# Gates by tanh, two layer norms applied on another engine, a second head copied by VectorE, and loops in another order

## What is computed

```python
x = x + attn(layernorm(x), Wq, Wk, Wv, Wo)           # the 16 heads of one token attend to each other
x = x + xattn(layernorm(x), ctx, Wq, bq, Wkv, bkv, Wp, bp)
#   q, k rounded per head to 127 steps, v per column, softmax over all 2048 keys,
#   probabilities rounded to 255 steps; 16 heads x 2048 queries x 2048 keys
x = x + moe(layernorm(x), gate, expert_bias, w1, w2, w3, shared_w1, shared_w2, shared_w3)
#   scores = sigmoid(x @ gate.T); the 2 of 8 experts with the largest score + bias
#   out = shared expert + sum over the chosen experts of w2(silu(w1 x) * (w3 x))
```

## Time and profile before

| what | value |
|---|---|
| time, median of 3 runs | 1123.94 us (1122.27 to 1124.36) |
| the profiled execution | 1121.76 us, of which its span is 1119.9 us |
| first scores kept (end of set-up) | 92.3 us |
| one tile in the steady part | about 63.1 us |
| VectorE, ScalarE, GpSimd, TensorE busy | 84%, 81%, 79%, 80% |
| mean granted TensorE clock | 0.98 |

### The profile page before, as it was taken

How to read it: one execution, slowest core, us unless ns; L and a number is a source line. 1 busy time by engine, 2 the same in 40 slices (tenths; PEclk the granted TensorE clock), 3 DMA queues, 4 the chain that set the end, 5 groups by cost and what they waited for, 6 DMA issues and landing times.

```text
span 1119.9 us, 30149 instructions
## 1 busy us (share of the span) xinstructions
PE 890.8 (80%) x11283; PEld 616.6 (55%) x11424; DVE 936.5 (84%) x1817; ACT 911.9 (81%) x1085; POOL 883.4 (79%) x890
## 2 busy tenths in 40 slices
PE   7956778787887878787887878787887878788786
PEld 4543446565555656565555556565655556556455
DVE  4967788888988888888988888898988888898883
ACT  2646889888888889888888889888888989889892
POOL 7669978897979888898979889898979888854040
PEclk9976999999999999999999999999999999999998
DMA  6011000000000000000000000000000000000000
GB/s 215 2 38 43 6 2 6 1 7 7 6 6 7 6 7 6 2 6 7 6 7 6 7 1 12 1 7 6 7 6 6 7 2 6 2 6 2 6 2 11
DMA packets 8438, 14.00 MB, mean 12 GB/s; under 512 B 1635, under 2 KB 6246, under 8 KB 7910
## 3 DMA queue, kind: packets, MB, share of 16 engines
q1 hardware_dynamic: 8294, 12.06, 3.2%
HBM read 9.96 MB, written 2.10 MB: 11 GB/s over the span
## 4 chain that ended last, share of the span: by engine, by line
PE 41%; issue 17%; ACT 15%; DVE 13%; POOL 12%; POOLq 1%; DMA 0%; DVEq 0%; SPq 0%; ACTq 0%
PE ps_score L1445 10%; PE ps_score L1456 9%; DVE score L1087 8%; PE ps L1310 7%; ACT prob L791 6%; ACT prob_t L803 5%; PE ps_pv L1472 4%; POOL routed_both L508 3%; PE ps L1519 2%; POOL gate L464 2%; PE ps_score L1310 2%; ACT queries L776 2%; POOL folded L545 1%; PE ps L1398 1%; PE ps L1549 1%
## 5 line engine op out<-in xcount | busy, mean ns | idle before, releaser
L1087 DVE TENSOR_SCALAR_CACHE_REDUCE score<-ps_score,q_neg 128x1024 f32<-128x1024 f32 x512 | 644.7, 1281 | 73.5 <-PE ps_score L1445 66.4
L791 ACT ACTIVATE prob<-score,exp_bias 128x2048 uint16<-128x2048 f32 x256 | 514.0, 2008 | 16.5 <-DVE exp_bias L1097 16.4
L1445 PE MATMUL ps_score<-keys,queries 128*128 128x512 bf16 x883 | 276.1, 382 | 114.9 <-ACT prob_t L803 73.2
L803 ACT COPY prob_t<-ps_score 128x1024 int32<-128x1024 int32 x240 | 242.8, 1012 | 80.5 <-PE ps_score L1456 77.8
L1456 PE MATMUL ps_score<-ident_f,prob 128*128 128x128 f16 x4096 | 272.1, 220 | 33.9 <-issue 30.0
L1456 PEld LDWEIGHTS ps_score<-ident_f,prob 128*128 128x128 f16 x4096 | 239.4, 98 | 96.5 <-issue 73.0
L545 POOL TENSOR_TENSOR folded<-product 128x512 f32<-128x512 f32 x128 | 161.7, 1271 | 42.9 <-DVE hs L1023 33.9
L1445 PEld LDWEIGHTS ps_score<-keys,queries 128*128 128x128 bf16 x1024 | 70.8, 97 | 201.1 <-issue 151.7
L535 POOL TENSOR_TENSOR product<-hs_exp,v_tok 128x1024 f32<-128x1024 f32 x64 | 149.0, 2350 | 14.0 <-ACT hs_exp L759 14.0
L535 POOL TENSOR_TENSOR product<-qk_rot 128x1024 f32<-128x1024 f32 x64 | 149.3, 2344 | 0.2 <-POOL qk_rot L528 0.2
L553 POOL TENSOR_TENSOR folded<-folded 128x256 f32<-128x256 f32 x128 | 92.2, 738 | 0.0
(11 more groups left out here) (144 smaller groups left out, 1225.6 us busy)
## 6 DMA issues: line engine op xcount, KB each, us to landing
prob_t<-in_w SPq DMA_DIRECT2D x3, 1024.0 KB, 4.8
x_in<-in_x SPq DMA_DIRECT2D x16, 128.0 KB, 2.0
score<-in_cond_t SPq DMA_DIRECT2D x4, 512.0 KB, 6.5
out<-x_out SPq DMA_DIRECT2D x16, 128.0 KB, 1.7
w_qkv<-in_w_qkv SPq DMA_DIRECT2D x1, 768.0 KB, 4.1
early<-in_w_kv SPq DMA_DIRECT2D x1, 512.0 KB
w_s<-in_w_s SPq DMA_DIRECT2D x3, 128.0 KB
w_o<-in_w_o SPq DMA_DIRECT2D x1, 256.0 KB
```

The costliest lines, as they stand in the source:

```text
L791: act.activation(prob[:, s, :].bitcast(U16), score[:, s, :], ACT.Exp, bias=exp_bias[:, s:s + 1], scale=-1.0, accum_out=prob_sum[:, t.par, ...
L803: act.copy(prob_t[:, t.count(H, h) % KEPT].rearrange("p k q -> p (k q)").bitcast(I32), ps_score[:, slot(h + TURN, 2)].rearrange("p b k -> ...
L1087: dve.tensor_scalar(score[:, s, HALF * i:HALF * i + HALF], ps_score[:, slot(h, i)].rearrange("p b k -> p (b k)"), q_neg[:, t.par, h:h + 1] ...
L1445: mm = pe.matmul(ps_score[:, slot(h, i), b, :], queries[:, t.par, h // 2, h % 2, :], keys[:, h // 2, k0:k0 + KEYS], start=True, stop=True)
```

## The change

Five things are changed.

1. **Norms.** `POOL_NORMS = (0,)`: for kinds 1 and 2 GpSimd no longer applies the norm. It makes a third one-column value, `shift` = -mean x rstd, and ScalarE applies the norm (`ln_apply`, `activation(Identity, scale=rstd, bias=shift)`). `ln_apply(2)` stands at h = 8, `ln_apply(1)` at h = 10.
2. **Gates.** ScalarE takes tanh(z/2); GpSimd makes the sigmoid as 0.5 tanh + 0.5, one instruction in place of an addition and a power. `choose` has 12 instructions instead of 13, `choose_last` one less.
3. **Copies.** `DVE_KEEPS = (9, 13)`: VectorE also copies the turned probabilities that come due at place 9 (head 7); ScalarE copies 14 a tile, not 15.
4. **Loop order.** All four bodies are written in another order.
5. **Set-up order.** Queries of the first tile are made before the last keys are turned. On VectorE the second half of the value maxima and the scaling of the values stand before the last keys' low parts. VectorE copies the first two quarters of the turned values, ScalarE the last two.

```diff
-DVE_KEEPS = (13,)
+POOL_NORMS = (0,)
+DVE_KEEPS = (9, 13)
...
+                if kind not in POOL_NORMS:
+                    pool.tensor_scalar(shift[:, kind:kind + 1], mean_var[:, kind, 0:1],
+                                       rstd[:, kind:kind + 1], -1.0, ALU.mult, ALU.mult
+                        ).then_inc(ln_shifted[kind], 1)
+                    return
...
+            def ln_apply(kind, t):
+                act.wait_ge(ln_shifted[kind], t.count(1, 1))
+                if kind > 0:
+                    act.wait_ge((one_done, two_done)[kind - 1], t.count(1, 1))
+                if (due := t.due(1)) is not None:
+                    act.wait_ge(ln_turned[kind], due)
+                x = (x_in[:, t.par, :], x_one[:, t.par, :], x_two[:])[kind]
+                act.activation(normed[:, kind, :], x, ACT.Identity, bias=shift[:, kind:kind + 1],
+                               scale=rstd[:, kind:kind + 1]).then_inc(ln_done[kind], 1)
...
-                pool.tensor_scalar(gate_exp[:], gate_exp[:], 1.0, None, ALU.add).then_inc(gate_chain, 1)
-                pool.wait_ge(gate_chain, t.count(13, 1))
-                pool.sem_inc(settled, 1)
-                pool.tensor_tensor(sig, gate_exp[:], minus_one[:].to_broadcast([P, E]), ALU.pow).then_inc(gate_chain, 1)
+                pool.tensor_scalar(sig, gate_tanh[:], 0.5, 0.5, ALU.mult, ALU.add).then_inc(gate_chain, 1)
...
-                act.activation(gate_exp[:], bank[5][:, 0:E], ACT.Exp, scale=-1.0).then_inc(gate_exped, 1)
+                act.activation(gate_tanh[:], bank[5][:, 0:E], ACT.Tanh, scale=0.5).then_inc(gate_tanhed, 1)
...
                 if m.exists() and t.exists():
                     route(0, m)
                 if a.exists():
                     fold_more(3, a)
+                    shift_scores(a)
                 if m.exists() and t.exists():
                     route(1, m)
                 if a.exists():
-                    shift_scores(a)
...
+                if u == T // 2 - 1:
+                    reduce_values(1, first)
+                    value_maxima(1)
                 if 1 <= u <= T // 2:
                     rest_of_keys(u - 1)
+                if u == T // 2 - 1:
+                    scale_values()
```

More of the change, by code:

```diff
@@ L287, in layer_kernel @@
         ln_stat = [sem(f"ln_stat{i}") for i in range(3)]
+        ln_shifted = [sem(f"ln_shifted{i}") for i in range(3)]
         ln_scaled = [sem(f"ln_scaled{i}") for i in range(3)]
@@ L404, in ln_scale @@
                 pool.sem_inc(settled, 1)
+                if kind not in POOL_NORMS and (due := t.due(1)) is not None:
+                    pool.wait_ge(ln_done[kind], due)
+                    pool.sem_inc(settled, 1)
                 pool.tensor_scalar(var_eps[:, kind:kind + 1], mean_var[:, kind, 1:2], EPS, None, ALU.add
@@ L579, in body @@
                     ln_scale(0, a)
+                if m.exists():
+                    spread_sums(m)
                 if n.exists():
@@ L589, in body @@
                     fold_more(G + 3, n)
+                if n.exists() and not t.starts():
+                    norm_ho(n)
                 if a.exists():
@@ L593, in body @@
                     norm_ho(n)
-                if n.exists() and not t.starts():
-                    norm_ho(n)
+                if m.exists():
+                    ln_scale(2, m)
                 if a.exists():
@@ L908, in _ @@
                     head_exp(first)
+                if u == 5 and 0 not in POOL_NORMS:
+                    ln_apply(0, second)
                 if u == 6:
@@ L913, in _ @@
                     keep_qkv(1, second)
+                if u == 8:
+                    keep_ho(first)
                 if u == 9:
-                    keep_ho(first)
+                    if 1 not in POOL_NORMS:
+                        ln_apply(1, first)
+                    ln_keep(1, first)
                 keys_and_values(u)
-            keep_one(first)
-            ln_keep(1, first)
-            keep_values(0)
-            keep_values(1)
             keep_queries(first)
@@ L1192, in body @@
                 for h in range(H):
+                    if n.exists() and h == 9 + late:
+                        dve.wait_ge(ho_projected, n.count(1, 1))
+                        ln_gather(1, one_bank(n)[:, 0:D], n)
+                        ln_combine(1, n)
                     if n.exists() and h == 13 + late:
@@ L1618, in body @@
                         turn(H + h - TURN, m)
-                    if m.exists() and h == 13:
-                        spread_gates(1, m)
-                    if n.exists() and h == 6 + late:
-                        ho_turn(n)
                     if m.exists() and h == 4:
```

301 lines of the change are left out of this document (154 added, 147 removed).

## The result

The changed kernel takes 1081.03 us in the median (1080.8 to 1081.26, 4 runs), the kernel before 1124.05 in the same runs. The ratio is 0.962, 95% interval 0.9604 to 0.9637. The forecast was 1090.9 with a range of 1074 to 1110: direction and range held, the gain was 43 us where 33 had been worked out. The profiled execution of after has a span of 1078.9 us against 1119.9, so 41.0 us are to be accounted for.

A forecast was written before the change was run, and what follows sets the result against it. Waits between four engines about 80% busy bound the kernel, with GpSimd late. Tiles 1 to 13 -31.2, other tiles +1.2, set-up -2, tail -1.1 sum to -33.1: 1088.7 profiled, 1090.9 median; range 1074 to 1110.

The forecast's parts named there:

- The reading of tile 14: Heads 12 to 14: tile 14, GpSimd mostly idle, shows late GpSimd's waits; their going gives -3.4 us a tile.
- The sum for the gates: GpSimd ahead of `choose`: 3.9 less work, 2.5 wait and 1.3 fold gone; gates 4.7 to 7.7 us earlier.
- Rival C: GpSimd asks too early for the third norm's statistics, so everything behind slips and it gets slower, about 1137; chance 0.07.
- 0.3 for what tile 14 lacks: Steady tiles also have `reduce_scores(1)` and `largest_score` at place 14: +0.3 us a tile, ends 0 and 0.9.
- ScalarE at 0: ScalarE gets 1.2 us of norms, loses a 1.0 us copy, within 8 us idle a tile: 0 us.
- The second copy at +0.4: VectorE's second copy of a turned head costs +0.4 us a tile, between 0 and +0.8.
- `shift_scores` at +0.3: Tile's end: subtraction ahead of `route(1)` makes the way by GpSimd and TensorE longer, +0.3 us a tile, ends 0 and 1.6.
- The shift's margin: Second norm's `shift` is ready between 2 us before ScalarE wants it at place 10 and 2 us after.
- Set-up: -2 forecast: Set-up: GpSimd's 2.31 us norm becomes 0.6 on ScalarE, last keys slip beside quantisation; -2 us, ends +1 and -5.
- Tail: -1.1 forecast: Last tile: third norm as shift plus apply gives about -0.9 us, a reciprocal less in `choose_last` 0.20; together -1.1.
- Rival B: Head loop also shortens around heads 0 and 11, subtraction's detour costs nothing: 3.6 us a tile, 1075; chance 0.09.
- the route way: Tile's end: path by GpSimd's subtraction, `route(1)`, experts and scores, 4.2 us against VectorE's 3.9; +0.3 us a tile.

The follow-up runs named there:

- before_tanh: Kernel before with only the gates' power on GpSimd replaced by the tanh form; 1099.15 us, ratio 0.9781.
- before_light: Kernel before with tanh gates and GpSimd's second and third norms cut to 16 of 256 columns from tile 1 on; 1086.43 us, ratio 0.9668.
- before_pool_order: Kernel before with only GpSimd's work in a tile put in the changed kernel's order; 1156.26 us, ratio 1.0288.
- one_copy: Changed kernel with VectorE copying one turned head (place 13) instead of two, ScalarE copying that of place 9 again; 1094.7 us, ratio 0.9747.
- shift_last: Changed kernel with GpSimd's subtraction of the self-attention's maximum (shift_scores) put behind route(1) again; 1079.95 us, ratio 0.9619.
- pad_before_shift: Changed kernel with one useless GpSimd operation a tile (0.89 us) ahead of the second norm's scale and shift; 1081.58 us, ratio 0.9631.
- setup_old: Changed kernel with the kernel before's set-up order on TensorE, ScalarE and VectorE, second norm still on ScalarE; 1082.0 us, ratio 0.9636.
- before_order_fixed: Kernel before with GpSimd's new order, but rope ahead of norm_ho and the third norm's statistics at place 6; 1150.67 us, ratio 1.0243.
- after_old_pool_order: Changed kernel with GpSimd's work in a tile in the order of the kernel before; 1136.99 us, ratio 1.0115.

## Why the prediction was right, and where it was off

**The reading of tile 14: right.** The natural experiment gave -3.4 us for the waits of heads 12 to 14; they gave 3.6. That GpSimd's lateness is the cause is shown by before_tanh and before_light, which take work from GpSimd and from nothing else.

**The sum for the gates: right, but its parts don't stand alone.** 4.7 to 7.7 us sooner were forecast and 5.4 came, and in the changed kernel the parts are there: the wait of 2.46 us is gone, the third fold is behind `choose`, and GpSimd waits 2.2 us for VectorE's sums (1.95 at `ho`, 0.26 at `sum_inv`), where up to 3 was allowed. But 3.7 of the 7.7 were put down to the order as a thing of its own. before_pool_order shows that by itself the order brings the gates later, at 51.9 us of the tile instead of 50.3. What failed is the step that added order and removed work as if each could be had without the other.

**Rival C: the mechanism is real, the kernel misses it.** It said that GpSimd would ask too soon for the third norm's statistics. In after `var_eps` follows `rope` without a wait, and the shift is 5.4 us ahead of ScalarE. In before_pool_order it waits 2.08 us; there the statistics still come at place 7. What C didn't name is `x_two`, the longer wait.

**0.3 for what tile 14 lacks: not paid.** Heads 12 to 14 take 12.44 us, the same three in tile 14 of after 4.96 + 4.02 + 3.36 = 12.34. The term was 0.1.

**ScalarE at 0: the price was right, the balance wrong.** 0.6 for an applied norm is what the rows show. But I held the copy that goes, 1.0, and the norms that come, 1.2, against 8 us of idle time in a tile. one_copy shows that at places 9 and 10 there is none to spare.

**The second copy at +0.4: wrong sign.** Its direct price was right, +0.47 at place 9, but in this kernel it saves 13.7 us. The step that failed is the lower end: 0, with the argument that a slot is released sooner. It should have been below nothing, since ScalarE had just got work at that place (that this is the reason is argued: no run has the copy without the norms). In the sum the miss doesn't show as 1.3 us a tile (13.7 us over 16 tiles and the 0.4), because the prediction had not charged ScalarE with its norms either: two errors of opposite sign, and that they cancel is luck. Places 8 to 11 cost 0.64 us instead of 0.4.

**`shift_scores` at +0.3: 0.05**, by shift_last and by place 15 (4.31 to 4.36). The order of the two ways was right, their distance was not.

**The shift's margin: right.** "Between 2 us before and 2 us after" was 0.64 us before. pad_before_shift shows that some 0.15 us beyond it still cost nothing.

**Set-up: -2 forecast, +0.08 measured.** The term took GpSimd's norm of 2.31 us in the earlier trace rows at its face. It costs 1.24 elsewhere; the rest was time beside VectorE's long operations, and with the old set-up order that stayed behind on GpSimd's shift, as setup_old shows. With the new order the norm did come 2 us sooner, and the step that failed is the overlap: the last keys' turns and copies were to slip beside the quantisation of the queries at no cost, and TensorE was still at them when the queries were ready. Whether the new order is better than the old one with the same norm is not shown: 1082.0 against 1081.03, and the intervals overlap.

**Tail: -1.1 forecast, -1.2 measured, in part by luck.** The norm gave 0.2 of its 0.9: from VectorE's `mean_var` to its first operation on the gates it was 1106.47 - 1101.25 = 5.22 us and is 1066.24 - 1061.20 = 5.04. The reciprocal gave its 0.2. From `routed_gate` to the first product of the experts' second layer 0.5 more went, which I had not listed, and that is no work saved: TensorE spreads the gates with a granted clock of 0.53 before (1107.9 to 1112.0) and of 0.83 in the changed kernel (1067.6 to 1071.5).

```profile
1107.93 3.78 PE L1519 MATMUL ps<-ident,routed_gate 128*128 128x128 f32 x16
```
```profile
1067.69 2.54 PE L1555 MATMUL ps<-ident,routed_gate 128*128 128x128 f32 x16
```

**The whole.** Against the forecast of the sum, -33.1, the profile has -41.0: tiles 1 to 13 gave 8.65 more (0.67 a tile: 0.25 at the subtraction, 0.5 at heads 12 to 14, 0.1 at place 0, less 0.24 at places 8 to 11), tiles 0, 14 and 15 1.2 more, the set-up 2.1 less. Rival B's time, 1075, was nearer in size, but only one part of its mechanism came true, that the route way costs nothing: places 0 to 11 did not get shorter, they take 0.5 us more. The other marks held: GpSimd 51.6 us a tile, no wait for `routed_gate` or the fold, steps 0 to 11 within 1 us in all. The distance between tiles was to be 60.7 and is 59.95; VectorE was to be busy 56 us and is 55.6.

Open is what the other reordered steps (TensorE's products at heads 0 and 11) gave: places 12 and 13 are 0.2 and 0.1 us shorter than in before_light, but no run changes them alone.

## What to carry to other kernels

Take a stretch of the same trace where an engine has little to do as the measure of what its lateness costs: here it gave the gain at heads 12 to 14 within 6%. When work moves from one engine to another, list what the remaining piece still waits for, as well as its duration; an order that is good for the new piece can be bad for the old one, and neither edit need be worth anything alone. And hold the price of moved work against the idle time at its own place in the loop, never against the idle time of a whole tile.

## What the runs showed of the hardware that I had not expected

**A stall of TensorE can cost twice.** In the windows of tiles above the granted clock of the changed kernel is 1.00. In before_order_fixed TensorE waits 2.40 us for the gates, and its clock in the stretch behind that is 0.70 of 2.4 GHz, a mix of the two levels 1.2 and 2.4: the spread of the gates takes 2.07 us instead of 1.11. In after_old_pool_order it is 0.56 behind ScalarE's stall. one_copy shows it within one kernel. The same wait of 1.56 us is followed by a clock of 1.00 in the tile that begins at 519.33 and by 0.64 in the one at 580.0, and place 10 takes 4.66 us in the first and 6.29 in the second. So the losses of the slower kernels above are not waits alone; how much of them is clock, no run separates. The windows are, in this order, one of before_order_fixed, one of after_old_pool_order and two of one_copy.

```profile
600.35:606.00 5.65, 5.57 (x35) 4.61 (x36) 1.91 (x3) 3.49 (x5) 5.65 (x5) 0.70 0.01 4
```
```profile
649.00:656.00 7.00, 5.03 (x25) 3.58 (x27) 3.64 (x8) 5.99 (x9) 4.04 (x13) 0.56 0.01 1
```
```profile
617.20:622.00 4.80, 4.80 (x43) 4.12 (x46) 2.13 (x5) 3.73 (x7) 3.98 (x7) 0.64 0.00 2
...
556.00:560.00 4.00, 3.47 (x63) 3.12 (x68) 2.74 (x7) 3.99 (x8) 3.43 (x6) 1.00 0.01 4
```

**A GpSimd operation of one input can cost more than its columns.** 256 columns times a constant took 0.885 us, 768 columns 2.164, which is 2.5 ns a column and some 0.25 us fixed; the applied norm, 256 columns with two operands of one value a partition, took 1.24. VectorE took 0.45 us for 256 columns with one such operand, ScalarE 0.60 with two. The norm also does two operations where the other row does one, and no run here has two with constants at this width; at 128x8 GpSimd took 0.20 us for two with constants and 0.24 for one, so I put the difference down to the operands, which is argued and not shown. The prediction had weighed the rule of "GPSIMD Engine Reference", "Engine selection", in the Trainium skill, that one input runs there roughly at line rate. The operation with a constant comes nearer to it than the norm, at twice VectorE's 0.45.

**Small operations of GpSimd can stand 2 us beside long ones of VectorE,** and the other way round: in the set-up of after VectorE's scaling of `w_p` took 4.07 us where it took 0.8 before, with two products of GpSimd, 4.66 us in all, running from 78.84 on.

```profile
79.58 4.07 DVE L1036 TENSOR_SCALAR w_p<-w_p,v_scale 128x256 f32<-128x256 f32 x2
```
